# The four steps of the softmax shift, moved from one burst on VectorE to one behind each of four maxima

## The reference

```python
xn = _layernorm(x, axis=-1)
x = x + attention(xn, w_qkv, w_out, b_out, mask_logits) + ffn(xn, W_fc, W_proj)

# attention: 16 heads of 16; q and k pass a spectral filter
scores = jnp.einsum('bhqd,bhkd->bhqk', q, k) / math.sqrt(dh)
attn = jax.nn.softmax(scores, axis=-1)
out = jnp.einsum('bhqk,bhkd->bhqd', attn, v)

# ffn: h = relu(x W_fc')^2, y = h W_proj', five steps of a leaky threshold unit on y,
# the mean of its spikes
```

## Time and profile before

| | |
|---|---|
| three runs, median | 1758.84 us (1754.17 to 1760.1) |
| the profiled execution, its time | 1755.41 us |
| its span | 1753.6 us |
| TensorE busy | 1634.4 us, 93% |
| VectorE busy | 1506.6 us, 86% |
| ScalarE busy | 1177.1 us, 67% |
| GpSimd busy | 787.4 us, 45% |
| mean granted TensorE clock | 0.977 |
| longest of the waits of L806 for `delta_sb` | 3.0 us |

### The profile page before, as it was taken

The page is one execution under the profiler, slowest core; times in us unless marked ns, Lnnn a source line. Parts: engine busy times, 40 slices in busy tenths (PEclk is TensorE's granted clock), DMA queues, the critical chain, the costliest instruction groups (busy, mean ns, idle before and its releaser), DMA issues.

```text
span 1753.6 us, 60281 instructions
## 1 busy us (share of the span) xinstructions
PE 1634.4 (93%) x24366; PEld 1220.9 (70%) x24366; DVE 1506.6 (86%) x2782; ACT 1177.1 (67%) x2274; POOL 787.4 (45%) x1075
## 2 busy tenths in 40 slices
PE   9998999999999999999899999999999999999898
PEld 6566677677677677777676776776766776767677
DVE  7887898888898889889898898988988888889784
ACT  5546677677676677667676676776776676777572
POOL 2103345555444455555444455554344555544344
PEclk9999999999999999999999999999999999999999
DMA  6761233233222332333222323332223233322423
GB/s 225 231 224 47 69 87 82 66 87 83 80 67 71 84 80 71 83 85 82 68 74 75 84 65 84 85 84 73 68 76 85 70 78 86 83 69 73 134 58 100
DMA packets 150776, 156.83 MB, mean 89 GB/s; under 512 B 74464, under 2 KB 113248, under 8 KB 150496
## 3 DMA queue, kind: packets, MB, share of 16 engines
q1 hardware_dynamic: 147040, 149.75, 31.1%
q10 hardware_dynamic: 3456, 3.21, 0.6%
HBM read 119.80 MB, written 27.79 MB: 84 GB/s over the span
## 4 chain that ended last, share of the span: by engine, by line
PE 62%; DVE 16%; SPq 13%; DMA 4%; issue 3%; ACT 2%; ACTq 0%; POOL 0%; DVEq 0%; POOLq 0%
PE banks L821 22%; PE ring L773 14%; DVE pmax L1032 11%; PE ring L806 10%; PE banks L831 6%; SPq L361 4%; DMA delta_sb<-delta_scratch 4%; PE banks L826 3%; SPq L351 3%; DVE shift L1055 2%; SPq L371 2%; SPq L335 2%; ACT probs L626 2%; PE ring L942 2%; SPq L317 1%
## 5 line engine op out<-in xcount | busy, mean ns | idle before, releaser
L626 ACT ACTIVATE probs<-ring 128x512 f32<-128x512 f32 x2048 | 1076.0, 601 | 485.2 <-PE ring L806 303.7
L1032 DVE TENSOR_REDUCE pmax<-ring 128x1 f32<-128x512 f32 x2000 | 1246.5, 681 | 106.6 <-PE ring L773 98.1
L773 PE MATMUL ring<-kst,qst 64*128 64x512 f32 x2000 | 812.6, 451 | 42.3 <-DVE pmax L1032 42.3
L806 PE MATMUL ring<-qst,delta_sb 64*128 64x512 f32 x1664 | 607.9, 454 | 58.0 <-DMA delta_sb<-delta_scratch 56.4
L821 PE MATMUL banks<-probs,vst 128*32 128x128 f32 x16384 | 564.8, 279 | 0.0
L821 PEld LDWEIGHTS banks<-probs,vst 128*32 128x32 f32 x16384 | 424.1, 111 | 141.9 <-ACT probs L626 99.2
L773 PEld LDWEIGHTS ring<-kst,qst 64*128 64x128 f32 x2000 | 376.8, 188 | 180.2 <-issue 99.8
L806 PEld LDWEIGHTS ring<-qst,delta_sb 64*128 64x128 f32 x1664 | 283.1, 189 | 122.1 <-DMA delta_sb<-delta_scratch 69.8
L826 PE MATMUL banks<-xnT,wfc_sb 64*128 64x128 f32 x2016 | 279.5, 281 | 1.5 <-ACT relu_sb L631 1.5
L826 PEld LDWEIGHTS banks<-xnT,wfc_sb 64*128 64x128 f32 x2016 | 275.2, 197 | 4.9 <-ACT relu_sb L631 1.9
L831 PE MATMUL banks<-wproj_sb,hid_sb 64*128 64x256 f32 x1024 | 263.3, 377 | 0.0
(11 more groups left out here) (97 smaller groups left out, 1113.4 us busy)
## 6 DMA issues: line engine op xcount, KB each, us to landing
kst<-qk_scratch SPq DMA_DIRECT2D x256, 128.0 KB, 2.7
qst<-qk_scratch SPq DMA_DIRECT2D x256, 128.0 KB, 2.9
delta_sb<-delta_scratch SPq DMA_DIRECT2D x256, 64.0 KB, 1.9
tail<-qk_scratch SPq DMA_DIRECT2D x512, 26.0 KB, 2.2
delta_sb<-delta_scratch SPq DMA_DIRECT2D x128, 80.0 KB, 2.1
qk_scratch<-attnT SPq DMA_DIRECT2D x32, 256.0 KB, 3.0
shift_rows<-shiftT SPq DMA_DIRECT2D x512, 2.0 KB
delta_scratch<-tail SPq DMA_DIRECT2D x256, 26.0 KB, 2.0
```

The lines of the kernel that those rows point to most:

```text
L626: act.activation(probs[:, g % PS, :], score_bank(g), ACT.Exp, scale=SCALE).then_inc(exp_done, 1)
L773: pe.matmul(max_bank(x), qst[b][rows, tile * P:(tile + 1) * P], kst[b][rows, chunk * BLK:(chunk + 1) * BLK], start=True, stop=True).then_i ...
L806: pe.matmul(score_bank(g), delta_sb[rows, at:at + P], qst[b][rows, q:q + BLK], start=False, stop=True, skip_group_check=True).then_inc(sco ...
L1032: dve.tensor_reduce(pmax[:, tile, chunk:chunk + 1], max_bank(x), AX, ALU.max).then_inc(mx_taken, 1)
```

## The change

The four steps are no longer called in one loop behind one maximum. The late shift's links go behind the maxima m = 16, 17, 18 and 19, one each, and the early shift's behind m = 48, 49, 50 and 51. Link 1 is an addition of `nmax` and the zeros in columns 16 to 23 of `shift`, with the same rounded output, in place of the cast. The wait for the zeros moves from link 3 to link 1 of the first shift. The first shift of all, ahead of the units, is still made in one piece.

```diff
                 if link == 1:
                     dve.wait_ge(max_step, 2 * n + 1)
-                    dve.tensor_copy(shift[:, 0:8].bitcast(F32R), nmax[:]).then_inc(max_step, 1)
+                    if n == 0:
+                        dve.wait_ge(shift_blank, 1)
+                    dve.tensor_tensor(shift[:, 0:8].bitcast(F32R), nmax[:], shift[:, 16:24], ALU.add).then_inc(max_step, 1)
...
                     if n:
                         dve.wait_ge(shift_in, SHIFT * n)
-                    else:
-                        dve.wait_ge(shift_blank, 1)
                     dve.transpose(shiftT[:], shift[:]).then_inc(shift_turned, 1)
...
-                if m == LEAD - 1:
-                    for link in range(4):
-                        split_shift(link, 2 * i + 1, 1, CHUNKS * (i + 1))
+                if 0 <= m - LEAD < 4:
+                    split_shift(m - LEAD, 2 * i + 1, 1, CHUNKS * (i + 1))
...
-                if m == MINI // 2 + LEAD - 1 and not last:
-                    for link in range(4):
-                        split_shift(link, 2 * i + 2, 0, CHUNKS * (i + 1) + CHUNKS // 2)
+                if 0 <= m - LEAD - MINI // 2 < 4 and not last:
+                    split_shift(m - LEAD - MINI // 2, 2 * i + 2, 0, CHUNKS * (i + 1) + CHUNKS // 2)
```

## The result

The changed kernel took 1795.84 us (median of 4 runs, 1794.48 to 1798.32) beside 1756.51 for the kernel before (median of 4). The ratio is 1.0224, with a 95% interval from 1.0199 to 1.025: **slower by 39 us**. The forecast was 1810, slower, with a range of 1778 to 1845.

The account below looks back on a forecast made before the run. The prediction took TensorE to be bound by the early shift through SyncE's queue to the delta load, and by VectorE's bursts. 61 lost, 35 gained and 29 lost make 55 us on 1755.4: about 1810, range 1778 to 1845.

Parts of the forecast that it names:

- The early turn: VectorE's end of the shift for the next unit's first half; SyncE's copies, keys, moves and delta loads queue behind it.
- Lateness: Early turn and SyncE's work behind it 2.2 us later in 31 passages, 68 us, less 7 us hidden: 61 us lost.
- the steps between them, 0.55: Extra VectorE time, 0.55 us, for the four shift steps set between four maxima, part of the early turn's 2.2 us delay.
- SyncE's own lateness: In some twelve passages SyncE reaches the copies after the turn anyway, hiding 0.6 us on average, 7 us in all.
- The saving: Late burst costs TensorE 1.29 us; spreading it gains 1.2 us in 29 of 32 units: 35 us gained.
- The clock: Lower granted clock behind TensorE's longer delta wait: loss rises from 0.95 to 1.9 us in 31 stretches, 29 us lost.
- the rows of 3.0 and 5.5 us: Profiled TensorE waits of those lengths, with clock losses of 1.4 and 2.5 us behind them; the forecast took 1.9 between.
- The additions didn't wait: Rival in the early place: addition and subtraction wait for GpSimd, turn 0.9 us later, 28 us more, 1838; chance 0.2.
- the row at 1686.89: Profile row: a two-SBUF-input VectorE instruction inside GpSimd's TENSOR_SCALAR took 0.28 us, as in quiet places; so no wait counted.
- The clock did cost more: Answers the rival that the longer wait for delta adds no clock loss, giving 1781; chance 0.12.
- The kernel wasn't faster: Answers the rival that the later turn is absorbed before the delta load, leaving 55 us of savings, 1700; chance 0.05.
- The 2.3 us cover it: Late shift's turn comes about 1.5 us later; SyncE reaches its copies 2.3 us after the turn, so nothing was counted.

Follow-up runs that it names:

- the early shift alone: Against the kernel before, only the early shift's steps are spread, with the addition; the late shift stays one burst with its cast: 1833.9 us, ratio 1.0444.
- the late shift alone: Against the kernel before, only the late shift's steps are spread, with the addition; the early shift stays one burst with its cast: 1750.4 us, ratio 0.9948.
- late shift alone, moves on ScalarE: Against the kernel before, only the late shift is spread, the addition is in both, and ScalarE issues the output's moves: 1667.1 us, ratio 0.9483.

## Why the prediction was right, and where it was not

**The sign and the way.** The early turn lies on the path through SyncE's queue: 33 waits of L361, the first copy 0.03 us behind the turn, and the early shift alone costs 78 us (4.44%). Every sign that the prediction named for this came: L806's wait of 124 us (120 to 140 named), L773's of 1.0 (under 10), over 25 waits of L361, 30 of 31 stretches at a clock of 0.85 or below.

**The terms.** Lateness: 61 us forecast; measured 31 x 2.02 - 29 x 0.25 = 55. The term "the steps between them, 0.55" was mis-sized: a step adds 0.08 us and not 0.14. SyncE's own lateness, 7 us, was right. The saving: 35 forecast, 29 x 1.34 = 39 measured; nothing of the late burst was left to lose. The clock: 29 forecast, 30 measured (29 x 1.02 and 0.9 in the unit before the last; the first stretch became 1.2 shorter, which the wait at step 32 behind it swallowed). That size was in part luck. The forecast took the loss to grow with the wait, between the rows of 3.0 and 5.5 us, but in the kernel after the stretch behind the longest wait, 4.98 us, took 11.56 us at 0.83, and one behind a wait of 3.5 us 12.08 at 0.79; and the kernel before already had two stretches of 12.6 and 12.7 us at 0.75 behind waits of 2.6 us. And a term that the sum didn't have: SyncE's stretch from copy to resumption was 0.22 us shorter, 6 us. Some 4 of the 6 are waits of SyncE for exponentials inside the stretch, which the later copies mostly find met: 7.4 us in units 1 to 29 before, 3.5 after. The rest isn't settled; the stretch scatters from 13.4 to 14.8 us in either kernel. 55 - 39 + 30 - 6 = 40, against 55 forecast: lateness, saving and this term all came out on the cheaper side.

**The rivals.** The additions didn't wait. The addition started 0.03 us ahead of L524, and the subtraction ran inside it at 0.16 us, as the row at 1686.89 had it. The clock did cost more. The kernel wasn't faster.

**What the prediction had wrong without paying for it.** "The 2.3 us cover it", of the late shift: on average 0.56 us was left of 3.06 in the kernel before, and in four of 29 units the late copies followed their turn by 0.03 us. And it treated the parts as terms of one sum. They aren't: the late shift alone gains 9 us and the early one alone loses 78, which makes 69, and together they lose 39. The saving shows in full only where the loss has made room.

## What to carry to other kernels

Where one engine's queue takes part in every cycle, find all the loops through it and their lengths before pricing an edit: a wait that is shortened in one comes back in the next, and a saving counts only down to the length of the second longest loop. Spreading small steps between larger ones was nearly free here for the engine that does them, but the last one's consumer gets it later by the whole spread; ask for each result separately who waits for it. A transfer's issue that is moved off the fullest queue can be worth much though no engine works less: here 94 us for eight issues per unit, four of them in each loop.

## What the runs showed of the hardware that was not expected

- A small step on VectorE between two maxima of 0.68 us costs 0.08 us, though it is listed with 0.16 to 0.20 (kernel after, the passage at 571.83 to 574.68).
- An addition with two SBUF inputs waits for GpSimd's TENSOR_TENSOR as a cast does (652 and 654 ns on average in the bursts). Inside GpSimd's TENSOR_SCALAR (L524) a subtraction of that kind took 0.16 us in each of the 31 early shifts of the kernel after.
- A transfer issued by ScalarE lies beside its own activation and didn't hold it up here (late shift alone, moves on ScalarE):

```profile
587.76 0.59 ACTq L638 DMA_DIRECT2D attnT<-o_turned  x1
587.82 1.24 ACT L623 ACTIVATE probs<-ring 128x512 f32<-128x512 f32 x2
```
